# Row maxima of a windowed attention handed over by group of heads, in a fused model block on one core

## What is computed

```python
xn = layernorm(x)
x = x + favor(xn) + local(xn)        # favor: 16 heads of random features, causal
xn = layernorm(x)                    # local: 2 layers, each 8 heads of 64, then a gated unit
x = x + attention(xn) + experts(xn)  # attention: 16 heads of 8; 8 experts, top 2, and a shared one

# in each of the two local layers
q, k = rotary(l2norm(q) * qs), rotary(l2norm(k) * ks)
sim  = 8 * q @ k^T                   # a query sees its own window of 64 and the one before, masked
attn = softmax(sim)
x    = x + (attn @ v) @ wo
```

## Time and profile before

| | us |
|---|---|
| median of 3 runs | 2316.77 |
| lowest and highest run | 2305.25, 2322.8 |
| the profiled execution, its own time | 2311.75 |
| its span, first to last instruction | 2310.0 |
| mean granted TensorE clock in it | 0.927 of full |
| PE busy / DVE busy / ACT busy / POOL busy | 1905.3 / 1303.9 / 743.8 / 291.6 |

### The profile page before, as it was taken

One profiled execution on the slowest core, in us unless ns is written; L12 is line 12 of the kernel. 1 busy time (PEld: TensorE's weight loads), 2 busy tenths in 40 slices (PEclk: granted clock), 3 DMA queues, 4 the chain that ended last, 5 costly groups with the idle time before them and its releaser, 6 DMA issues.

```text
span 2310.0 us, 46813 instructions
## 1 busy us (share of the span) xinstructions
PE 1905.3 (82%) x19804; PEld 1122.4 (49%) x19836; DVE 1303.9 (56%) x2957; ACT 743.8 (32%) x1353; POOL 291.6 (13%) x234
## 2 busy tenths in 40 slices
PE   1788797888888798878988879888798887988878
PEld 1455454464454544545445455364554554545544
DVE  1556546655466564666536565365655565556564
ACT  0322252323422235223252232513334223432234
POOL 0110101101011021010210111101111011011010
PEclk9999899988999999998999989999899998999989
DMA  4000200002000020000200001000100002000020
GB/s 166 1 2 2 32 7 2 1 2 33 7 2 1 2 33 7 2 1 5 29 7 2 1 12 23 6 2 2 22 13 6 2 2 32 3 6 2 2 28 7
DMA packets 27491, 29.88 MB, mean 13 GB/s; under 512 B 3524, under 2 KB 25844, under 8 KB 26740
## 3 DMA queue, kind: packets, MB, share of 16 engines
q1 hardware_dynamic: 27284, 26.88, 6.2%
HBM read 11.93 MB, written 2.36 MB: 6 GB/s over the span
## 4 chain that ended last, share of the span: by engine, by line
PE 56%; DVE 23%; ACT 6%; SPq 4%; issue 4%; DMA 4%; ACTq 0%; DVEq 0%
PE bank L968 5%; SPq L415 4%; PE bank L882 4%; PE bank L674 4%; PE bank L702 4%; PE bank L872 3%; DMA phi<-parts 3%; PE bank L857 3%; DVE lmx L1303 3%; DVE lrec L1317 2%; PE bank L576 2%; PE bank L694 2%; PE bank L616 2%; PE bank L895 2%; DVE lc L1298 2%
## 5 line engine op out<-in xcount | busy, mean ns | idle before, releaser
L1474 DVE TENSOR_REDUCE amx<-bank 128x2 f32<-128x512 f32 x256 | 163.2, 686 | 77.2 <-PE bank L895 77.2
L1317 DVE RECIPROCAL lrec<-bank 128x256 f32<-128x256 f32 x64 | 112.3, 1755 | 135.8 <-PE bank L722 134.8
L1106 ACT ACTIVATE silu<-bank 128x512 f32<-128x512 f32 x144 | 84.2, 597 | 276.6 <-PE bank L857 264.5
L1463 DVE TENSOR_TENSOR mh<-bank,silu 128x512 f32<-128x512 f32 x144 | 98.8, 691 | 111.8 <-PE bank L872 105.0
L452 POOL TENSOR_TENSOR lc<-lc,ls 128x512 f32<-128x512 f32 x32 | 40.8, 1276 | 940.6 <-DVE lc L1267 940.6
L882 PEld LDWEIGHTS bank<-w_mw,mh 128*128 128x128 f32 x1152 | 145.0, 203 | 22.5 <-issue 22.5
L882 PE MATMUL bank<-w_mw,mh 128*128 128x128 f32 x1152 | 152.4, 290 | 0.0
L857 PE MATMUL bank<-xn2T,w_mw 128*128 128x512 f32 x288 | 144.4, 625 | 0.0
L616 PE MATMUL bank<-hT,w_wqkv 128*128 128x512 f32 x256 | 122.3, 616 | 12.0 <-ACT lsq L1035 6.2
L1303 DVE TENSOR_REDUCE lmx<-bank 128x4 f32<-128x512 f32 x128 | 79.6, 685 | 69.5 <-PE bank L674 69.5
L1493 DVE RECIPROCAL ftm<-bank 128x256 f32<-128x256 f32 x16 | 28.1, 1758 | 149.8 <-PE bank L968 149.8
(11 more groups left out here) (268 smaller groups left out, 3833.1 us busy)
## 6 DMA issues: line engine op xcount, KB each, us to landing
phi<-parts SPq DMA_DIRECT2D x96, 64.0 KB
lc<-parts SPq DMA_DIRECT2D x96, 64.0 KB
w_mw<-in_mw SPq DMA_DIRECT2D x3, 1152.0 KB
x_in<-in_x SPq DMA_DIRECT2D x8, 256.0 KB, 9.8
out<-res SPq DMA_DIRECT2D x8, 256.0 KB, 2.3
w_wqkv<-in_wqkv SPq DMA_DIRECT2D x1, 1536.0 KB
w_w<-in_w SPq DMA_DIRECT2D x1, 682.0 KB
mh<-in_rotary SPq DMA_DIRECT2D x1, 512.0 KB
```

Source lines behind the costliest of these rows:

```text
L1317: V.reciprocal(lrec[:, k % 2, :], bank_of("loc_den", k)[:, 0:SEQ]).then_inc(sem["loc_rec"], 1)
L1463: V.tensor_tensor(mh[:, n % 4, :], bank_of("moe_u", n)[:], silu[:, n % 2, :], ALU.mult).then_inc(sem["moe_h"], 1)
L1474: V.tensor_reduce(amx[:, 2 * b:2 * b + 2, h], bank_of("att_max", n)[:].rearrange("p (t k) -> p t k", t=2), AX.X, ALU.max).then_inc(sem["at ...
```

## The change

In the local layers:

- The quad in slot "nmT" (its product on PE) now stands between the scores of group 0 and those of group 1, no longer behind both.
- DVE negates the maxima of each group as soon as its four reductions are done; `lnm` and `lnmT` have a place for each group. In group 1 the reductions run in the order i = 3, 0, 1, 2.
- There are two transposes of maxima a layer, `maxima_rows(0)` ahead of the first step and `maxima_rows(1)` ahead of the third, and two copies on ACT, one ahead of the Exps of steps 0 and 2.
- The steps run by group and then by batch: `g, b = divmod(n, 2)`. `wo` of batch 0 so waits for the third product of DVE, that of batch 1 for the fourth.
- Banks: group 0's maxima are in the ring "quad", group 1's in [4, 5, 6, 0] (layer 0) or [4, 5, 7, 0] (layer 1), the transposes in "norm". All later jobs of these rings move with that.

Beside it, to make room: `wT` lies in `lrT`, and `moe` is gone: x1 takes its sum in place, and ACT's copy of x_in to x1 waits for "result" of the turn before (it waited for "moe_base").

```diff
-    "loc_max_ps": 16, "loc_nmT_ps": 2, ...
+    "loc_max_ps": 16, "loc_nmT_ps": 4, ...
-        lnm = sb("lnm", [P, TT, 4, 32], BF16)
-        lnmT = sb("lnmT", [P, T], BF16)
+        lnm = sb("lnm", [P, 2, TT, 4, 32], BF16)
+        lnmT = sb("lnmT", [P, 2, T], BF16)
-        wT = sb("wT", [3 * EX, T], BF16)
+        wT = lrT[0:3 * EX, :]
-        moe = sb("moe", [P, TT, D])
...
-        RINGS = {"short": range(0, 6), "long": range(6, 8), "quad": range(0, 4), "norm": range(4, 8),
+        RINGS = {"short": range(0, 6), "long": range(6, 8), "quad": range(0, 4), "norm": range(4, 8), "wide": [4, 5, 6, 0], "wide1": [4, 5, 7, 0],
...
-                   ... "loc_pv": "norm", "favor_out": "norm"}
+                   ... "loc_pv": "norm", "loc_nmT": "norm", "favor_out": "norm"}
...
-            ring = "long" if (name, k) in LONG else RING_OF[name] if name in RING_OF else "short"
+            ring = ("quad", "wide", "quad", "wide1")[k // 4] if name == "loc_max" else "long" if (name, k) in LONG else RING_OF[name] if name in RING_OF else "short"
...
-                    job("loc_max", 8 * l + 4 * g + i, "loc_mx", 8 * l + 4 * g + i + 1)
-            job("loc_nmT", l, "loc_nmT", l + 1)
+                    job("loc_max", 8 * l + 4 * g + i, "loc_mx", 8 * l + 4 * g + (i if g == 0 else (i + 1) % 4) + 1)
+            job("loc_nmT", 2 * l, "loc_nmT", 2 * l + 1)
             for n in range(5):
                 k = 4 * l + n
+                if n == 2:
+                    job("loc_nmT", 2 * l + 1, "loc_nmT", 2 * l + 2)
...
# PE
-                    favor_heads(l, "nmT")
-                    pe.wait_ge(*freed("loc_nmT", l))
-                    o = bank_of("loc_nmT", l).bitcast(BF16)
-                    pe.wait_ge(sem["loc_nm"], now("loc_nm", l + 1))
+                        if g == 0:
+                            favor_heads(l, "nmT")
+                    def maxima_rows(g):
+                        pe.wait_ge(*freed("loc_nmT", 2 * l + g))
+                        o = bank_of("loc_nmT", 2 * l + g).bitcast(BF16)
+                        pe.wait_ge(sem["loc_nm"], now("loc_nm", 2 * l + g + 1))
...
+                    maxima_rows(0)
...
-                        b, g = divmod(k % 4, 2)
+                        g, b = divmod(k % 4, 2)
...
-                        if k % 4 == 0:
-                            pe.wait_ge(sem["loc_nmT"], now("loc_nmT", l + 1))
+                        if k % 2 == 0:
+                            pe.wait_ge(sem["loc_nmT"], now("loc_nmT", 2 * l + g + 1))
...
+                        if n == 2:
+                            maxima_rows(1)
                         if n < 4:
                             loc_sT(k)
...
-                        pe.wait_ge(sem["loc_o"], now("loc_o", 2 * n + 2))
+                        pe.wait_ge(sem["loc_o"], now("loc_o", 4 * l + 3 + b))
...
# ACT
-                act.wait_ge(sem["moe_base"], prior("moe_base"))
+                act.wait_ge(sem["result"], prior("result"))
...
                     for k in range(16 * l, 16 * l + 16):
+                        if k % 8 == 0:
+                            g = k // 8 % 2
+                            act.wait_ge(sem["loc_nmT_ps"], now("loc_nmT_ps", 2 * l + g + 1))
+                            A(lnmT[:, g, :], bank_of("loc_nmT", 2 * l + g)[:, 0:256].bitcast(BF16), ACT.Copy).then_inc(
+                                sem["loc_nmT"], 1)
...
# DVE
-                        for h in range(4 * g, 4 * g + 4):
+                        for i in range(4) if g == 0 else (3, 0, 1, 2):
+                            h = 4 * g + i
...
-                    dve.wait_ge(sem["loc_mx"], now("loc_mx", 8 * (l + 1)))
...
+                        dve.wait_ge(sem["loc_mx"], now("loc_mx", 8 * l + 4 * g + 4))
+                        mx = lmx[:].rearrange("p j i g -> p (j i) g")[:, :, g]
+                        hi, lo = [lnm[:, g].rearrange("p j i s -> p (j i) s")[:, :, s] for s in range(2)]
+                        link(V.tensor_scalar(hi, mx, -1.0, None, ALU.mult))
+                        V.scalar_tensor_tensor(lo, mx, -1.0, hi, ALU.mult, ALU.subtract).then_inc(sem["loc_nm"], 1)
                     dve.wait_ge(sem["favor_pv"], now("favor_pv", 4 * l + 4))
                     favor_out(l)
...
-                V.tensor_tensor(moe[:], x1[:], by_row(5), ALU.add).then_inc(sem["moe_base"], 1)
+                V.tensor_tensor(x1[:], x1[:], by_row(5), ALU.add).then_inc(sem["moe_base"], 1)
```

More of the change, by code:

```diff
@@ L47 @@
     "x_kept": 1, "xnT": 1, "hT": 4, "favor_qk": 2, "favor_sq": 2, "favor_phi": 8,
-    "loc_sq": 16, "loc_ss": 2, "loc_rT": 2, "loc_v": 8, "loc_nmT": 2, "loc_p": 32,
+    "loc_sq": 16, "loc_ss": 2, "loc_rT": 2, "loc_v": 8, "loc_nmT": 4, "loc_p": 32,
     "glu_h": 8, "glu_sq": 2, "glu_gain": 1, "glu_gate": 6,
@@ L247, in build @@
                    "route_T": "seven", "moe_g": "seven", "moe_w": "seven", "moe_u": "seven", "att_max": "seven",
-                   "att_nmT": "seven", "xnT": "five", "favor_qk": "five", "favor_v": "acc", "att_v": "acc", "att_sT": "five", "loc_pv": "norm", "favor_out": "norm"}
+                   "att_nmT": "seven", "xnT": "five", "favor_qk": "five", "favor_v": "acc", "att_v": "acc", "att_sT": "five", "loc_pv": "norm", "loc_nmT": "norm", "favor_out": "norm"}
         turns_of = {n: 0 for n in RINGS}
@@ L678, in _ @@
                                             ins.then_inc(sem["loc_max_ps"], 1)
-                    favor_heads(l, "nmT")
-                    pe.wait_ge(*freed("loc_nmT", l))
-                    o = bank_of("loc_nmT", l).bitcast(BF16)
-                    pe.wait_ge(sem["loc_nm"], now("loc_nm", l + 1))
[L683 to L687, removed]
+                        if g == 0:
[4 more added lines that the diff above has]
+                        pe.wait_ge(sem["loc_nm"], now("loc_nm", 2 * l + g + 1))
+                        for j in range(TT):
+                            last = nc.tensor.transpose(o[:, j * P:(j + 1) * P],
+                                                       lnm[:, g, j, :, :].rearrange("p i s -> p (i s)"),
+                                                       W["ident4"][:, 0:P])
+                        last.then_inc(sem["loc_nmT_ps"], 1)
+                    maxima_rows(0)
                     def loc_sT(k):
-                        b, g = divmod(k % 4, 2)
+                        g, b = divmod(k % 4, 2)
                         t = b * SEQ
@@ L709, in loc_sT @@
                                 r = slice(32 * i, 32 * i + 32)
-                                ins = mm(bank_of("loc_sT", 4 * k + i)[:, c0:c0 + nq], W["nmrow"][r, g, :],
-                                         lnmT[r, t + q0:t + q0 + nq], start=False, stop=True, skip_group_check=True)
+                                ins = mm(bank_of("loc_sT", 4 * k + i)[:, c0:c0 + nq], W["nmrow"][r, 0, :],
+                                         lnmT[r, g, t + q0:t + q0 + nq], start=False, stop=True, skip_group_check=True)
                                 if kt == 1:
@@ L1115, in _ @@
                 act.wait_ge(sem["route_T_ps"], now("route_T_ps", 1))
-                A(wT[:], bank_of("route_T")[0:3 * EX, 0:256].bitcast(BF16), ACT.Copy).then_inc(sem["route_T"], 1)
+                A(wT, bank_of("route_T")[0:3 * EX, 0:256].bitcast(BF16), ACT.Copy).then_inc(sem["route_T"], 1)
                 widen(1)
@@ L1300, in _ @@
                     for g in range(2):
-                        for h in range(4 * g, 4 * g + 4):
+                        for i in range(4) if g == 0 else (3, 0, 1, 2):
+                            h = 4 * g + i
                             dve.wait_ge(sem["loc_max_ps"], now("loc_max_ps", 8 * l + h + 1))
-                            V.tensor_reduce(lmx[:, :, h % 4, g], bank_of("loc_max", 8 * l + h)[:].rearrange("p (j k) -> p j k", j=TT),
+                            V.tensor_reduce(lmx[:, :, i, g], bank_of("loc_max", 8 * l + h)[:].rearrange("p (j k) -> p j k", j=TT),
                                             AX.X, ALU.max).then_inc(sem["loc_mx"], 1)
-                    dve.wait_ge(sem["loc_mx"], now("loc_mx", 8 * (l + 1)))
-                    mx = lmx[:].rearrange("p j i g -> p (j i) g")
-                    hi, lo = [lnm[:].rearrange("p j i s -> p (j i) s")[:, :, s:s + 4:2] for s in range(2)]
-                    link(V.tensor_scalar(hi, mx, -1.0, None, ALU.mult))
-                    ins = V.scalar_tensor_tensor(lo, mx, -1.0, hi, ALU.mult, ALU.subtract)
-                    ins.then_inc(sem["loc_nm"], 1)
+                        dve.wait_ge(sem["loc_mx"], now("loc_mx", 8 * l + 4 * g + 4))
[3 more added lines that the diff above has]
+                        V.scalar_tensor_tensor(lo, mx, -1.0, hi, ALU.mult, ALU.subtract).then_inc(sem["loc_nm"], 1)
                     dve.wait_ge(sem["favor_pv"], now("favor_pv", 4 * l + 4))
@@ L1314, in _ @@
                         k = 4 * l + n
[L1315 removed]
+                        g, b = divmod(n, 2)
                         dve.wait_ge(sem["loc_den"], now("loc_den", k + 1))
@@ L1498, in _ @@
```

(2 more changed lines are left out.)

9 lines of the change are left out of this document (3 added, 6 removed).

## The result

The changed kernel takes 2351.98 us (median of 4 runs, 2350.7 to 2353.02) against 2318.4 us of the kernel before (4 runs, 2305.25 to 2322.8): a ratio of 1.0154, with a 95% interval from 1.0112 to 1.0196. The profiled execution of it took 2350.7 us, with a span of 2348.9 and a mean granted clock of 0.913; before it was 2310.0 and 0.927. So the span grew by 38.9 us.

A forecast was written before the change was run, and what follows sets the result against it. The prediction saw no engine full: each turn is nearly one line of dependent steps. Layer 0's -10, the clock's -4 and layer 1's +44 us sum to +30, giving 2347 us on the median; range 2318 to 2370.

The forecast's parts named there:

- The bank of the transposes: Layer 1: group 0's transposes get bank 6, held until favor_out(1) ends on DVE; +2.05 us each layer 1.
- The rival in which favor_out(1) is no hurdle: Layer 1 gains as layer 0 does, transposes starting after two reductions; 2293 us, chance 0.05.
- The rest of layer 1: Layer 1 as a whole: later scores, bank wait and slower restart sum to +5.55 us, +44 over 8 turns.
- first reduction: Layer 1: scores wait for later scalings of lc, partly at the lower clock, so the first reduction is 1.3 us later.
- quad between the groups: Layer 1, as in layer 0: the quad's product delays group 1's scores and reductions by 0.7 us.
- masks and transposes at 0.50: Layer 1, restart behind PE's wait: masks and transposes at the lower clock take 1.7 us instead of 1.31, +0.4.
- L702 to Exp: Layer 1, first step: from its score products to the first Exp at the lower clock, +0.1 us over 2.66.
- first Exp to first den matmul: Layer 1, first step: 4.57 us in place of 3.17 in about half of the turns, +0.7.
- the rest, second transposes among it: Layer 1, ahead of the third step: the second group's transposes add +0.3 us.
- The main rival to the low side: Layer 1: clock holds through the wait, and layer 0's drops vanish; +1 us, 2318, chance 0.2.
- The rival to the high side: Low clock through most of layer 1: +53 us in all, 2370, chance 0.17.
- Layer 0: Layer 0: earlier transposes -1.05, masks -0.5, second transposes +0.3; -1.25 us a turn, -10 over 8, and -4 for clock drops.

The follow-up runs named there:

- Experiments 1: Changed kernel, with DVE running favor_out(1) in layer 1 between group 0's negation and group 1's reductions: 2293.12 us, ratio 0.9896 to the kernel before.
- experiment 2: Changed kernel, with layer 1's transposes of group 0 put in bank 4 and DVE's order kept: 2296.84 us, ratio 0.9916 to the kernel before.
- Experiment 5: The aliases alone: kernel before with only the room-making edits (moe in x1's place, wT in lrT, wait for result): 2316.71 us, ratio 1.0008.
- experiment 4: The filler: changed kernel plus 32 useless band-mask matmuls on PE ahead of layer 1's transposes: 2322.54 us, ratio 1.0033 to the kernel before.

## Why the prediction was right

**The bank of the transposes.** I put +2.05 on it, from PE having to wait for favor_out(1); the stretch from group 1's reductions to the transposes grew from 3.13 to 5.12, +1.99, in each layer 1. Experiments 1 and 2 show the cause from two sides. The rival in which favor_out(1) is no hurdle is out, and experiment 2 shows what it would have been worth: 2297, where I gave it 2293.

**The rest of layer 1**, +5.55 predicted, +5.45 measured, but the terms are less good than their sum:

| term | predicted | measured |
|---|---|---|
| first reduction | +1.3 | +1.67 |
| quad between the groups | +0.7 | +1.09 |
| favor_out's bank | +2.05 | +1.99 |
| masks and transposes at 0.50 | +0.4 | +0.30 |
| L702 to Exp | +0.1 | +0.38 |
| first Exp to first den matmul | +0.7 | -0.17 |
| the rest, second transposes among it | +0.3 | +0.19 |

The measured terms are differences of means over the eight turns; I had worked from turn 4. The first two are mis-sized by one thing. In turn 4 of before the low stretch of the clock around the scores ends 4.4 us behind the fourth scaling; after, with PE's pauses between the masks, it ends 8.6 behind it. So the scores of group 0 run at 0.50 throughout, and the quad's product behind them partly: 1.98 us (1048.18 to 1050.16) where I had counted 1.4. I had both cases only as the upper bound. The term from L702 to Exp came out larger because turn 4, against which I set it, was at 0.50 there; in three other turns before ran it in 1.53 us, at 1.00.

One term is wrong in sign. I took layer 0's 4.57 us of the earlier trace rows for the stretch from Exp to den in half of the turns; it was 3.17 in all eight. The low stretch begins while PE still waits (in turn 4 from 15.5 to 22.3 us behind the fourth scaling, with the transposes at 18.4 and the first Exp at 22.6), so much of it goes by in the wait itself, and the second step's L707 takes 1.38 us again. In the earlier trace rows it covered the Exps. The errors of the terms cancel.

**The clock.** The main rival to the low side, that the clock holds through the wait, failed in all eight turns. What it would have given can be told from the filler: C less by 1.78, so a run about 14 us shorter in layer 1, and 29 by the medians with what follows. With the clock held in the wait layer 1 so costs 3.7 us a turn (5.45 less 1.78), and not the 2.2 of that rival, which also had early scores and a faster first step than before. The rival to the high side, the low clock through most of layer 1, failed too: behind the wait it was at 0.50 for one step. But with the late scores the low level holds for 15.1 us of C's 42.4, against 7.6 of 36.95 before.

**Layer 0** was predicted at -1.25 with the transposes 6.4 us behind the first reduction; they stand 6.44 behind it. At the full clock A went from 34.82 to 33.41, -1.41: +0.73 for the quad, -1.78 from the reductions to the transposes (3.13 to 1.35), -0.58 for the masks, and +0.22 left, the second transposes. The three drops of before are all gone, worth -7.2 in all, where I took -4.

**What I had not.** Outside A and C the sum said nothing changes. It changed by +13.8: B -7.0, D +15.4, start and tail +5.4. On the profiled execution I had 2342, and it came to 2350.7; A was 4.5 better and C 0.4 better than summed, so all of the miss of 9 lies here. That the median came out within 5 us of my 2347 is in part luck. My errors have opposite signs, and what added the 13.8 was in no term of mine: without them I estimate 2338, slower still, but by 0.9%.

Two such stretches D of the kernel before, turns 5 and 6, with the same instructions (windows, columns as above):

```profile
1344.53:1510.24 165.71, 137.65 (x947) 76.34 (x950) 90.31 (x246) 63.21 (x107) 26.08 (x20) 0.91 0.10 14
...
1628.01:1786.46 158.45, 134.19 (x947) 73.92 (x950) 90.25 (x246) 63.25 (x107) 26.07 (x20) 0.92 0.08 15
```

One kernel runs the stretch in 158.45 and in 165.71, and two things differ. The first is the clock: 23.9 us at 0.50 in turn 6, 30.7 in turn 5. The second is a transfer. Ahead of L895 PE waits for copies of `parts` into `phi` that the DMA queue makes. In turn 5 that wait is

```profile
PE bank L895 <- DMA phi<-parts: 3.9, 1, 3.9
```

and in turn 6 there is none. The queue's packets, bytes and share of the 16 engines' span in turn 5 and in turn 6:

```profile
q1 hardware_dynamic: 2868, 2.16, 9.4%
...
q1 hardware_dynamic: 2868, 2.16, 7.5%
```

So the same packets took longer, an estimated 87 ns each against 66 (share times 16 times the stretch, over 2868). Of the 7.26 us between the two turns 3.8 are PE's waits for DMA. The clock alone doesn't tell such stretches apart: all seven D of the changed kernel have 30.7 us at 0.50, and they take 162.3 to 165.7, with 1.3 us of DMA waits in the shortest and 4.7 in the longest.

Before, D spent 25.8 us at 0.50 on the mean, after 30.7; PE's waits for DMA in it were 2.5 us, and 3.5 after. So about 1.0 of the +2.2 is the wait for the copies, and the rest goes with the clock; and the seven D of before lie between 158.5 and 165.7 by themselves, so that a mean of seven is uncertain by nearly 1 us. Over all 84 of these stretches, seven in each of the twelve kernels, D follows the time at 0.50 with a correlation of 0.78 and the DMA waits with 0.84. A fit by both gives 0.28 us for each us at 0.50 and 1.15 for each us waited, and leaves a scatter of 0.6 us where the stretches by themselves have 2.0. The tail spent 19.8 us at 0.50 and then 29.8, with DMA waits of 2.2 both times; its +4.25 so goes with the clock. These are correlations. Experiment 5 excludes the room-making edits, and experiment 4 moves D's time at 0.50 by an edit inside layer 1, but what in layer 1 decides whether a drop follows 50 us later was not shown, nor why the copies take longer in some turns, nor whether the change has a part in that. Nor did a run take apart B's -0.88; the kernels with the change's order are all between 44.67 and 45.28 there, the aliases alone give 45.42, before 45.76.

## What to carry to other kernels

When a result moves to another PSUM bank, look up in each round of the loop who held that bank, and where in its own program the engine that frees it stands: here one ring gave layer 0's transposes a bank that a reduction frees, and layer 1's one that favor_out frees, and layer 0 gained 1.4 us at the full clock where layer 1 lost 5.5. A product that nobody waits for is worth most behind the last work that others wait for, since there it covers an idle stretch, and the clock with it. Count a wait of the matmul engine twice: once for its length, once for what runs slower behind it.

## What the runs showed of the hardware

- The same unchanged stretch of about 160 us took between 158.4 and 166.4 us. The time that the granted clock was at its lower level in it ran from 20.5 to 34.1 us, and PE's waits for DMA copies in it from 0 to 4.8 us; the two together follow the time closely. The spread, 8.0 us a turn, is more than the whole loss in layer 1 (5.45), so a difference of about 1% in this kernel can come from there, and has to be looked for by stretches.
- The 2868 packets of one queue in that stretch, 2.16 MB, took 9.4% of the 16 engines' time in a turn of 165.71 us and 7.5% in one of 158.45 us, in the same execution.
- 32 small matmuls without any use, 4.52 us of them in a wait that stays, made the run 1.2% faster (ratio 1.0033 against 1.0154), and cost no time themselves: the transposes started 0.03 us earlier than without.
- The move of one product of 1.5 us, a matter of 0.6 us a layer, took the drops in layer 0 from three of eight turns to eight of eight, when PE's idle time went from 1.8 to 3.2 us. The change itself took them to none, at 1.5.
